# Cross-attention over fourteen context chunks: keys made five pieces ahead, the chunk loop written out, and the exponent ahead of the key copies on ScalarE

## The reference

```python
x = x + _L0_xattn_ref(_layernorm(x), ctx_1024, Wq, Wkv, Wo, bo)
...
q = x1 @ Wq                      # 128 x 1024
kv = x2 @ Wkv                    # x2: the context, 12544 x 256
k, v = jnp.split(kv, 2, axis=-1)
q, k, v = map(_split_heads, (q, k, v))
attn = jax.nn.softmax(jnp.einsum('bhid,bhjd->bhij', q, k) * SCALE, axis=-1)
out = jnp.einsum('bhij,bhjd->bhid', attn, v)
return out.reshape(b, l, h * d) @ Wo + bo
```

## Time and profile before

| | us |
|---|---|
| median of 3 runs | 1636.75 |
| lowest and highest | 1636.62, 1638.67 |
| the profiled execution's own time | 1637.99 |
| its span (the trace) | 1636.0 |

### The profile page before, as it was taken

One profiled execution on the slowest core, in us unless ns is written; L12 is line 12 of the kernel. 1 busy time (PEld: TensorE's weight loads), 2 busy tenths in 40 slices (PEclk: granted clock), 3 DMA queues, 4 the chain that ended last, 5 costly groups with the idle time before them and its releaser, 6 DMA issues. The chain is left out here.

```text
span 1636.0 us, 27278 instructions
## 1 busy us (share of the span) xinstructions
PE 1542.8 (94%) x10481; PEld 1448.6 (89%) x10481; DVE 1210.3 (74%) x2060; ACT 907.7 (55%) x1616; POOL 364.7 (22%) x166
## 2 busy tenths in 40 slices
PE   6999999999999999999999999999998789999569
PEld 6899999999999999999999999999986678888348
DVE  6788878887888788877888788888765436666764
ACT  5566666665666666666666566666541235555120
POOL 6503030303011111203030303010000236666230
PEclk9999999999999999999999999999998799999779
DMA  4201010000000010101010101000103511111600
GB/s 148 69 1 46 1 48 1 27 20 26 23 24 24 9 40 1 46 2 47 1 46 1 48 1 46 1 1 1 52 1 142 212 46 68 67 67 45 270 0 4
DMA packets 10356, 70.48 MB, mean 43 GB/s; under 512 B 2312, under 2 KB 2911, under 8 KB 8928
## 3 DMA queue, kind: packets, MB, share of 16 engines
q1 hardware_dynamic: 9198, 67.51, 11.2%
q10 hardware_dynamic: 1010, 1.07, 0.2%
HBM read 68.44 MB, written 0.13 MB: 42 GB/s over the span
## 5 line engine op out<-in xcount | busy, mean ns | idle before, releaser
L357 ACT ACTIVATE pTh<-ps 128x896 fp32r<-128x896 f32 x224 | 206.1, 920 | 365.8 <-PE ps L524 365.8
L399 DVE TENSOR_TENSOR K<-ps,K 64x448 fp32r<-64x448 f32 x448 | 278.8, 622 | 65.7 <-ACT K L332 62.2
L332 ACT CAST K<-ps 64x448 fp32r<-64x448 f32 x448 | 236.6, 528 | 76.3 <-PE ps L492 69.5
L404 DVE TENSOR_REDUCE nmx<-ps 128x1 f32<-128x896 f32 x224 | 242.7, 1083 | 13.4 <-issue 13.4
L433 DVE TENSOR_TENSOR pTl<-ps,pTh 128x896 fp32r<-128x896 f32 x224 | 244.5, 1091 | 5.8 <-ACT pTh L357 5.8
L550 PEld LDWEIGHTS ps<-cNh,pTh 128*128 128x128 f32 x1568 | 217.0, 190 | 14.3 <-issue 7.7
L550 PE MATMUL ps<-cNh,pTh 128*128 128x256 f32 x1568 | 224.9, 283 | 3.5 <-ACT pTh L357 3.4
L339 ACT ACTIVATE prob<-ps,nm 128x896 f32<-128x896 f32 x224 | 225.8, 1008 | 2.6
L550 PE MATMUL ps<-cNh,pTl 128*128 128x256 f32 x1568 | 224.8, 283 | 0.0
L550 PE MATMUL ps<-cNl,pTh 128*128 128x256 f32 x1568 | 224.6, 283 | 0.0
L263 POOL TENSOR_TENSOR cNh<-raw,zero 128x1792 fp32r<-128x1792 f32 x14 | 44.5, 3176 | 805.2 <-PE ps L550 795.5
(11 more groups left out here) (298 smaller groups left out, 1987.2 us busy)
## 6 DMA issues: line engine op xcount, KB each, us to landing
raw<-in_ctxT SPq DMA_DIRECT2D x14, 896.0 KB, 4.6
raw<-in_ctxN SPq DMA_DIRECT2D x14, 896.0 KB, 4.6
d_raw<-in_ctxT SPq DMA_DIRECT2D x14, 896.0 KB, 4.6
w<-in_w SPq DMA_DIRECT2D x2, 4096.0 KB, 18.0
wg<-in_wg SPq DMA_DIRECT2D x1, 4352.0 KB, 25.2
wu<-in_wu SPq DMA_DIRECT2D x1, 4352.0 KB, 17.9
wd<-in_wd SPq DMA_DIRECT2D x1, 4352.0 KB, 27.7
e_ea<-in_alog SPq DMA_DIRECT2D x1, 2048.0 KB, 8.1
```

What stands on the lines that cost most here:

```text
L332: nc.scalar.copy(K[halves[s], h, cols], ps[halves[s], piece_bank(g, first), 0:HK]).then_inc(sem("kh_ready"), 1)
L357: nc.scalar.activation(pTh[:, :], pT_ps, ACT.Copy).then_inc(sem("pTh_ready"), 1)
L399: ins = nc.vector.tensor_tensor(K[halves[1 - s], h, cols], ps[halves[s], piece_bank(g, first), 0:HK], K[halves[s], h, cols].bitcast(F32), ...
L404: nc.vector.tensor_reduce(nmx[:, :], S[u % 2], mybir.AxisListType.XY, ALU.max, negate=True).then_inc(sem("chunk_max"), 1)
```

## The change

Three edits, all in `stage_context`.

1. **Early keys.** Only five pieces (`AHEAD`) are made ahead of the loop; step u then makes piece u+5, across chunk boundaries, for steps 0 to 218. `K` keeps three pairs of heads in a ring (`RING`), so the copies also wait for `scores_done` of the pair that lay there.
2. **Written-out loop.** The hardware loops go; all 224 steps stand one after the other in each engine's stream. Since pieces go on until step 218, only two pairs of heads (`EARLY`) are turned and projected within the last four steps; the other six follow after the loop. `scale_sums` stands behind `U` in the odd steps of the last chunk. `UT` and `oT` have tiles of their own.
3. **Order on ScalarE.** The exponent of step u+1 is issued ahead of the copies of the piece.

```diff
-    steps = H0 * 2
-    last = pairs - 1
-    PIECES = H0
-    FIRST = 8
+    steps = H0 * chunks
+    AHEAD = 5
+    RING = 3
+    PAIRS = H0 // 2
+    EARLY = 2
...
-            K = sb("K", [P, H0, CK], F32R, loop)
+        K = sb("K", [P, 2 * RING, CK], F32R, keep)
...
 (ScalarE)
-                            act.wait_ge(sem("p_turned"), i * steps + (u + 1))
-                            nc.scalar.activation(pTh[:, :], pT_ps, ACT.Copy).then_inc(sem("pTh_ready"), 1)
-                            if makes:
-                                g = u % H0
-                                act.wait_ge(sem("piece_done"), i * steps + (PIECES * (u // H0 + 1) + g + 1))
-                                high_parts(g)
-                            if end and u + 1 == steps:
-                                break
-                            act.wait_ge(sem("max_done"), i * steps + (u + 2))
-                            act.wait_ge(sem("pv_free"), i * steps + (u + 2))
-                            exp_step(u + 1)
+                    act.wait_ge(sem("p_turned"), u + 1)
+                    nc.scalar.activation(pTh[:, :], pT_ps, ACT.Copy).then_inc(sem("pTh_ready"), 1)
+                    if u + 1 < steps:
+                        act.wait_ge(sem("max_done"), u + 2)
+                        act.wait_ge(sem("pv_free"), u + 2)
+                        exp_step(u + 1)
+                    p = u + AHEAD
+                    if p < steps:
+                        act.wait_ge(sem("piece_done"), p + 1)
+                        if p // 2 >= RING:
+                            act.wait_ge(sem("scores_done"), 2 * (p // 2 - RING) + 2)
+                        high_parts(p)
...
 (VectorE)
+                    p = u + AHEAD
+                    if p < steps:
+                        dve.wait_ge(sem("kh_ready"), 2 * p + 2)
+                        low_parts(p)
...
+                    if u >= steps - H0 and h % 2 == 1 and h < H0 - 1:
+                        scale_sums(h // 2)
+                scale_sums(PAIRS - 1)
+                for m in range(EARLY, PAIRS):
+                    outputs(m)
...
 (TensorE)
+                for p in range(AHEAD):
+                    if p >= 4:
+                        pe.wait_ge(sem("kl_ready"), p - 3)
+                    piece(p)
+                pe.wait_ge(sem("kl_ready"), 2)
+                pe.wait_ge(sem("ql_doubled"), 1)
+                scores(0)
+                scores(1)
...
+                    p = u + AHEAD
+                    if p < steps:
+                        if p % H0 == 0:
+                            pe.wait_ge(sem("cT_ready"), p // H0 + 1)
+                        pe.wait_ge(sem("kl_ready"), p)
+                        piece(p)
...
-                    with pe.Fori(0, last) as i:
-                        round_of(i, False)
-                    round_of(last, True)
...
+                turn(EARLY)
+                nc.tensor.matmul(ps[:, 0, 0:D], ones[0:1, :], v["brow"][0:1, 0:D], start=True, stop=False)
+                for m in range(PAIRS):
+                    if m == EARLY:
+                        turn(EARLY + 1)
+                    if m >= EARLY:
+                        project(m)
+                        if m + 2 < PAIRS:
+                            turn(m + 2)
+                    pe.wait_ge(sem("oT_ready"), m + 1)
+                    mm = nc.tensor.matmul(ps[:, 0, 0:D], oT[:, m, :], wo[:, m, :], start=False,
+                                          stop=(m == PAIRS - 1))
```

More of the change, by code:

```diff
@@ L182, in stage_context @@
     chunks = t["ctxN"].shape[0]
-    pairs = chunks // 2
-    steps = H0 * 2
-    last = pairs - 1
-    PIECES = H0
-    FIRST = 8
+    steps = H0 * chunks
+    AHEAD = 5
+    RING = 3
     SCALE = DH0 ** -0.5
     W = H0 * DH0
+    PAIRS = H0 // 2
+    EARLY = 2
     with ExitStack() as keep:
@@ new lines, in stage_context @@
+        flat = U[:, :, :].rearrange("p h d -> p (h d)")
+        wq = flat[:, 0:KT * W].rearrange("p (k n) -> p k n", k=KT)
+        wk = flat[:, KT * W:2 * KT * W].rearrange("p (k n) -> p k n", k=KT)
+        qh = sb("qh", [P, H0, P], F32R, keep)
+        ql = sb("ql", [P, H0, P], F32R, keep)
+        K = sb("K", [P, 2 * RING, CK], F32R, keep)
+        raw = sb("raw", [P, CK * KT], F32, keep)
+        rawT = raw[:, :].rearrange("p (k n) -> p k n", k=KT)
+        rawN = raw[:, :].rearrange("p (t d) -> p t d", t=NT)
@@ new lines, in stage_context @@
+        cTh = [sb(f"cTh{i}", [P, KT, CK], F32R, keep) for i in range(2)]
+        cTl = [sb(f"cTl{i}", [P, KT, CK], F32R, keep) for i in range(2)]
+        cNh = [sb(f"cNh{i}", [P, NT, D], F32R, keep) for i in range(2)]
+        cNl = [sb(f"cNl{i}", [P, NT, D], F32R, keep) for i in range(2)]
+        prob = sb("prob", [P, 2, HK], F32, keep)
+        pTh = sb("pTh", [P, CK], F32R, keep)
+        pTl = sb("pTl", [P, CK], F32R, keep)
+        nm = sb("nm", [P, 2, H0], F32, keep)
+        nmx = sb("nmx", [P, 1], F32, keep)
@@ new lines, in stage_context @@
+        al = sb("al", [P, 2], F32, keep)
+        rs = sb("rs", [P, 2], F32, keep)
+        rden = sb("rden", [P, H0], F32, keep)
+        wkh = sb("wkh", [P, KT, W], F32R, keep)
+        wkl = sb("wkl", [P, KT, W], F32R, keep)
+        wv = sb("wv", [P, KT, W], F32, keep)
+        wo = sb("wo", [P, PAIRS, D], F32, keep)
+        UT = sb("UT", [P, 2, 2, KT, P], F32, keep)
+        oT = sb("oT", [P, PAIRS, P], F32, keep)
+        S = [ps[:, 2 * i:2 * i + 2, 0:HK] for i in range(2)]
+        pT_ps = ps[:, 4:6, :].rearrange("p b n -> p (b n)")[:, 0:CK]
@@ new lines, in stage_context, with piece_bank, key_slot, piece_of @@
+        O = ps[:, 6, 0:D]
+        halves = (slice(0, DH0), slice(DH0, P))
+        def piece_bank(p):
+            return 4 + p % 4 if p < AHEAD else 7
+        def key_slot(h):
+            return 2 * ((h // 2) % RING) + h % 2
+        def piece_of(p, s):
+            return key_slot(2 * (p // 2) + s), slice((p % 2) * HK, (p % 2 + 1) * HK)
+        def turn_bank(m):
+            return 7 if m < EARLY else 6 + m % 2
+        def project_bank(m):
+            return 7 if m < EARLY else 4 + m % 2
```

615 lines of the change are left out of this document (274 added, 341 removed).

## The result

The changed kernel takes 1703.65 us (median of 4 runs, 1702.97 to 1708.81), against 1637.2 for the kernel before in runs on the same chip: a ratio of 1.0412, with a 95% interval of 1.0395 to 1.0428 (the two medians alone give 1.0406). It is 66 us slower. The forecast was 1725.5 in a range of 1686 to 1758. The profiled execution took 1702.97 with a span of 1701.2.

What follows compares the result with a forecast made beforehand. PE set the pace before; a VectorE-ScalarE ring of 5.75 us a step would after. Start, step 0, 218 ring steps, `scale_sums`, last five steps and end put `res` at 1339.9, +89 on the median: 1725.5 us, range 1686 to 1758.

Steps and rivals of the forecast that it cites:

- Early keys: Start of the sublayer: first transposes at 34.8 instead of 47.61, 12.8 us earlier, but not won.
- Written-out loop: Loop boundaries: a boundary step takes 6.94 us instead of 5.32, six times, so 10 us go; straight code costs nothing seen.
- `scale_sums`: Behind U in odd steps of the last chunk: 0.86 us, four times before the last piece, +3.4 us.
- the ring: Loop steps with a piece: VectorE and ScalarE wait for each other in a closed chain, 5.75 us against PE's 5.32.
- exponent to key copies: Link on ScalarE, start to start, not shown in the profile before: taken as 1.10 us.
- `den` to U: Link on VectorE without a wait, not shown before: between 0.19 and 0.31 us, taken as 0.27.
- The hole on PE: In front of the piece in the loop: PE waits 0.43 us a step for VectorE's low parts, 90 us in all.
- The other engines' waits: In the loop: VectorE waits some 300 us for key copies, none before U; ScalarE waits for `nm` before `al`.
- Step 0: First loop step: estimated 7.3 us, 5.75 plus 1.5 for matmuls still at the slow pace.
- The end: After the last step: six pairs turned and projected at 2.2 us each, 16.6 us in all, against 6.8 before.
- PE keeps the pace: Rival for the loop: steps stay at 5.32 us, total 1628.5 us, faster by 0.5%; chance 0.05.
- PE's clock falls too: Rival for the loop: the 0.43 us idle costs PE's full clock, steps of 6.65 us, total 1920; chance 0.04.

## Why the prediction was right, and where it was off

**What bounds the kernel, and the ring.** Right. The steps went to a ring of waits between VectorE and ScalarE, in the order forecast, and each of its links is in the rows after. Link by link, forecast and measured:

| from start to start | forecast | after |
|---|---|---|
| U to maximum | 0.40 | 0.40 |
| maximum to `nm` | 1.12 | 1.12 |
| `nm` to `al` | 0.25 | 0.25 |
| `al` to exponent | 0.20 | 0.20 |
| exponent to key copies | 1.10 | 0.99 |
| key copies to low parts | 1.11 | 1.10 |
| low parts to `den` | 1.29 | 1.29 |
| `den` to U | 0.27 | 0.29 |
| sum | 5.74, used as 5.75 | 5.64 |

**The term that was mis-sized** is the one that no row of before showed: exponent to key copies. The prediction bounded it by 1.00 and 1.12 and took 1.10, near the upper end, on the grounds that the read of the sum must have ended. The copies start when that read is half over, at +0.99, a hundredth below the least that the prediction allowed. With the rounding to 5.75 the ring was forecast 0.12 us above the average step of 5.63, and 218 x 0.12 = 26 us. That is more than the whole miss, 1339.9 against 1317.85 for `res` and 1725.5 against 1703.65 for the time, 22 us each: the terms below were forecast 4 us too short, and that it came out nearer is luck. `den` to U was the other unknown and was right within 0.02.

**The hole on PE.** Forecast 0.43 us a step and 90 in all, measured 0.30 and 59.7 in the wait table, since the ring is shorter. That the busy share would fall to 92% was wrong: it is 99% of the window. The prediction had read a PE row as time in which PE works.

**The other engines' waits.** VectorE for the copies: some 300 us forecast, 292 measured. ScalarE for `nm`: as forecast, 255 us. No wait in front of U: right, its matmuls end more than a microsecond before.

**Early keys.** Forecast first transposes at 34.8, measured 36.48. ScalarE waited 1.16 and 0.95 us for PE between the first key copies, where the rows of before had 0.65 once, so the scores began at 32.3 instead of 30.9, and half of them ran at the lower clock (0.37 us apart instead of 0.20). Step 0: 7.3 forecast, 6.93 measured. That the sooner start is not won was right, and the two kernels with written-out loops and the old order show it: with and without early keys they have the same time.

**Written-out loop.** 10 us forecast for the boundaries, 8.6 measured. The prediction multiplied by six; six rounds have five returns to the loop's start, and the trace has five long steps. The 10 us were not a term of the sum, which was built up from the steps of the changed kernel. No cost of straight code was seen.

**The end.** 16.6 us forecast, 18.0 measured (1317.85 less 1299.84, the last U's start less 0.2): 2.39 us a pair instead of 2.2, because from the product with `Wo` to the next projection it is 0.63 us (1307.56 to 1308.19) and not 0.45; the projection with the wait behind it took the 1.76 forecast. The prediction's own terms, 13.3 and 3, make 16.3 and not 16.6. The last five steps took 26.0 instead of 25.3.

**`scale_sums`.** It cost 0.85 us each time, as forecast, but it lies in the ring five times (steps 209 to 217), not four:

```profile
1251.54 0.48 DVE L463 SCALAR_TENSOR_TENSOR U<-U,al,ps 128x256 f32<-128x256 f32 x1
...
1257.17 0.48 DVE L463 SCALAR_TENSOR_TENSOR U<-U,al,ps 128x256 f32<-128x256 f32 x1
...
1263.65 0.48 DVE L463 SCALAR_TENSOR_TENSOR U<-U,al,ps 128x256 f32<-128x256 f32 x1
```

A step without it takes 5.63 us and one with it 6.48. Together start, step 0, last five steps, end and `scale_sums` were forecast 4.3 us too short (1.7 - 0.4 + 0.7 + 1.4 + 0.9), which hid a little of the error in the ring.

**The rivals.** "PE keeps the pace" would have been 1628.5. It did not come, but as the price of a kernel without the ring the number was right: with the old order the same kernel takes 1629.7. "PE's clock falls too" did not happen in the loop: 1.00 with a hole in every step. In the sublayer it was below 1.00 only in the first 50 us (0.50 from 34 to 39).

## What to carry to other kernels

Before moving an instruction on an engine with slack, follow the ring that it may close: each engine's own order counts as a link just as each semaphore does, and a ring that is longer than the bound engine's step becomes the pace, with both its engines idle for much of the time (here VectorE for 26% and ScalarE for 44% of the loop's window). The test is cheap: put an instruction of known length into the ring, or move one out of it into idle time. If 0.27 us moved gives 65 us over 218 steps, the ring is the bound; if an added one costs nothing, it is not.

## What the runs showed of the hardware

- On ScalarE the instruction after an exponent with a sum starts 0.99 us after it, when the exponent's row has just ended and the 0.19 us row of the sum's read is half over. `al` to exponent takes 0.20 us where `al` follows `pTh`, and 0.30 where it follows the key copies.
- Two small instructions on VectorE that don't depend on each other start 0.19 us apart though each row is 0.27 long.
- PE started at half its clock after a pause of 4.20 us, and at full clock after the pause was filled but for 0.76 us. After a pause of about 1.5 us that followed slow scores it was slow in the changed kernel (36.48), and so it was in five other versions with the same start (step 0 of 6.8 to 6.9 us), but at full pace in the profiled execution of the kernel with the old order (transposes at 36.80, the next at 42.14). There the scores were slow from the first one on, elsewhere from the third or fourth. What decides is open.
